# Scores gathered with the token rows, experts' inner rows weighted by them, and the six picked rows added without weights

## The reference, cut to what matters

```python
logits = xf @ w_router                     # 1024 tokens x 32 experts
scores = sigmoid(logits)
...                                        # 6 of 32 experts are picked by scores + corr_bias
# per picked expert e: y_e = (silu(x @ gate_w[e]) * (x @ up_w[e])) @ down_w[e]   (inner width 176)
# out = sum over the six picks of scores[e] * y_e, plus a shared expert (inner width 352)
x = x + gb * out
```

## Time and profile before

| | us |
|---|---|
| median of 3 runs | 437.58 |
| lowest, highest | 435.03, 437.88 |
| the profiled execution | 438.39 |
| span of its instructions | 436.6 |

### The profile page before, as it was taken

The page is one execution under the profiler, slowest core; times in us unless marked ns, Lnnn a source line. Parts: engine busy times, 40 slices in busy tenths (PEclk is TensorE's granted clock), DMA queues, the critical chain, the costliest instruction groups (busy, mean ns, idle before and its releaser), DMA issues. The chain is left out here.

```text
span 436.6 us, 6170 instructions
## 1 busy us (share of the span) xinstructions
PE 407.1 (93%) x1923; PEld 306.7 (70%) x1924; DVE 286.3 (66%) x693; ACT 201.8 (46%) x380; POOL 129.3 (30%) x143
## 2 busy tenths in 40 slices
PE   6996898988999999999999899899899979999997
PEld 6463748455777777777776647687587858798886
DVE  4898885887444444444444476989677998985542
ACT  2578825482222222222222247482896397613430
POOL 1000020004777777777777500701000010010000
PEclk9999696968999999999999989999999989999999
DMA  8996667981323233333238259902400000001001
GB/s 278 413 389 135 149 148 179 360 373 41 104 98 107 98 108 96 107 96 110 96 106 276 87 189 376 359 12 44 172 2 0 2 1 0 2 2 48 2 0 49
DMA packets 24010, 56.89 MB, mean 130 GB/s; under 512 B 4528, under 2 KB 15794, under 8 KB 22996
## 3 DMA queue, kind: packets, MB, share of 16 engines
q1 hardware_dynamic: 18564, 41.80, 28.7%
q0 software_dynamic: 5424, 14.82, 10.3%
HBM read 46.10 MB, written 10.50 MB: 130 GB/s over the span
## 5 line engine op out<-in xcount | busy, mean ns | idle before, releaser
L736 PE MATMUL bank<-arena,tile_mem 128*128 x224 | 75.6, 460 | 0.0
L1411 POOL DMA_INDIRECT tile_mem<-h_dram,gidx x57 | 56.0, 982 | 53.8 <-DVE gidx L1779 36.8
L1399 POOL TENSOR_TENSOR rstd<-ve,mhalf 128x2 f32<-128x2 f32 (+1 forms) x14 | 11.3, 806 | 185.9 <-DVE ve L1539 185.9
L1418 POOL DMA_INDIRECT y_dram<-norm,didx x56 | 55.3, 988 | 21.8 <-issue 13.7
L1795 DVE TENSOR_TENSOR tile_mem<-tile_mem,bank 128x176 f32<-128x176 f32 x56 | 18.9, 338 | 62.3 <-ACT tile_mem L1209 62.3
L752 PE MATMUL bank<-arena,tile_mem 88*128 x224 | 57.7, 379 | 0.8 <-DVE tile_mem L1790 0.8
L752 PEld LDWEIGHTS bank<-arena,tile_mem 88*128 88x128 f32 x224 | 42.4, 190 | 15.7 <-issue 1.0
L847 PE MATMUL bank<-x_r,f_r 128*128 128x512 f32 x192 | 46.4, 402 | 0.7 <-DVE x_r L1975 0.6
L736 PEld LDWEIGHTS bank<-arena,tile_mem 128*128 128x128 f32 x224 | 38.3, 191 | 11.8
L1209 ACT ACTIVATE tile_mem<-bank 128x176 f32<-128x176 f32 x56 | 17.8, 317 | 57.5 <-PE bank L736 57.5
L847 PEld LDWEIGHTS bank<-x_r,f_r 128*128 128x128 f32 x192 | 36.8, 193 | 9.8 <-issue 0.8
(11 more groups left out here) (281 smaller groups left out, 722.0 us busy)
## 6 DMA issues: line engine op xcount, KB each, us to landing
arena<-w_gu SPq DMA_DIRECT2D x3, 2112.0 KB, 12.3
arena<-w_dn SPq DMA_DIRECT2D x4, 1408.0 KB
arena<-w_gu SPq DMA_DIRECT2D x2, 2464.0 KB, 20.5
arena<-y_dram SPq DMA_DIRECT2D x6, 768.0 KB, 8.2
arena<-w_f SPq DMA_DIRECT2D x6, 512.0 KB, 7.8
arena<-wmod SPq DMA_DIRECT2D x3, 512.0 KB, 9.3
arena<-wmod SPq DMA_DIRECT2D x2, 768.0 KB, 11.0
arena<-y_dram SPq DMA_DIRECT2D x4, 384.0 KB, 4.5
```

Of the source, the lines that this page charges most:

```text
L736: mm = pe.matmul(bank[2 + r % 2][:, 0:2 * M], xgT[r % 2][:, k * P:(k + 1) * P], gu[:, bass.ds(e[k], 2 * M)], start=(k == 0), stop=(k == CT ...
L1411: pool.indirect_dma_start(out=xg[j % 4], out_offset=None, in_=h2_dram, in_offset=bass.IndirectOffsetOnAxis(ap=gidx[:, j:j + 1].bitcast(U32 ...
L1418: pool.indirect_dma_start(out=y_dram, out_offset=bass.IndirectOffsetOnAxis(ap=didx[:, j:j + 1].bitcast(U32), axis=0), in_=yt[j % 4], in_of ...
```

## The change

Five things, all in layer 0's mixture of experts:

1. A row of `h2_dram` is longer by 32 numbers: SP writes the 32 scores of each token behind its 256 channels with a second DMA per sequence, and what waits for h2 waits for both. A gather brings 288 numbers instead of 256.
2. `tile_hidden` becomes a scalar_tensor_tensor that also multiplies by the score of the tile's expert. That score is one column of the gathered row, and which column is held in a register: VectorE loads four registers from `eoff` at the head of each quad, as PE does.
3. A gather into a used buffer waits for `hid_ready` instead of `tx_done`, since the scores in it are read until then.
4. `wk`, its twelve instructions, ScalarE's `choice_parts` and PE's `choice_sums` go. VectorE adds the picked rows itself, without weights: for token tiles 0 and 1 together (`first_picks`, `other_picks`), for the others one tile at a time (`all_picks`).
5. SP reads the residual rows X2 ahead of its wait for the last scatter, not behind the picks.

Some buffers move (`pidx` and `pint` into others, the four `yg` buffers into one). The diff, cut to its core:

```diff
-    h2_dram = nc.dram_tensor("h2_dram", (B * S, C), F32, kind="Internal").ap()
+    h2_dram = nc.dram_tensor("h2_dram", (B * S, C + E), F32, kind="Internal").ap()
...
+                sp_.wait_ge(score_ready, b + 1)
                 sp_.wait_ge(h2_ready, b + 1)
-                sp_.dma_start(h2v[:, b * TB:(b + 1) * TB, :], norm[:, b * TB:(b + 1) * TB, :]).then_inc(h2_out, 16)
+                sp_.dma_start(h2v[:, b * TB:(b + 1) * TB, 0:C], norm[:, b * TB:(b + 1) * TB, :]).then_inc(h2_out, 16)
+                sp_.dma_start(h2v[:, b * TB:(b + 1) * TB, C:XR], scores[:, b * TB:(b + 1) * TB, :]).then_inc(h2_out, 16)
...
+            for b in range(B):
+                half = slice(b * TB * C, (b + 1) * TB * C)
+                sp_.dma_start(X2.rearrange("p t c -> p (t c)")[:, half], x1_dram[:, half]).then_inc(x1_in[b], 16)
             for i in range(4):
                 sp_.wait_ge(y_out[i], 16 * last_q + 16)
...
-            for t in range(TB):
-                choice_sums(t)
             pe.wait_ge(shhid_ready, 2 * SHT)
             shared_out(1, (2, 3), range(TB))
...
-            act.wait_ge(wk_ready, 1)
-            shared_silu(1, ms=range(2))
-            choice_parts(0)
-            choice_parts(1)
-            shared_silu(1, ms=range(2, SHT))
-            choice_parts(2)
-            choice_parts(3)
+            shared_silu(1)
...
                 if j >= 4:
-                    pool.wait_ge(tx_done, j - 3)
+                    pool.wait_ge(hid_ready, j - 3)
...
+            regs = [dve.alloc_register(f"score{i}") for i in range(4)]
             def tile_hidden(q, r):
+                e = dve.snap(regs[r], min_val=0, max_val=E - 1)
                 dve.wait_ge(sil_ready, 4 * q + (r + 1))
-                tt(hid[r % 2], sil[r % 2], bank[2 + r % 2][:, M:2 * M], ALU.mult).then_inc(hid_ready, 1)
+                stt(hid[r % 2], sil[r % 2], xg[r][:, bass.ds(e + C, 1)], bank[2 + r % 2][:, M:2 * M], ALU.mult, ALU.mult)\
+                    .then_inc(hid_ready, 1)
...
             def quad(q, first=False):
+                dve.load(regs, eoff[0:1, bass.ds(4 * q + 1, 4)])
                 for r in range(4):
...
+            def first_picks():
+                acc = shared_y[:, 0:2, :]
+                for t in range(2):
+                    dve.wait_ge(yg_half[t], 16)
+                for k in range(TOPK // 2):
+                    step(tt(acc, acc, yg_pair[:, :, k, :], ALU.add))
+                    settle()
...
+            def all_picks(t):
+                y, half = yg[t % YG], TOPK // 2
+                dve.wait_ge(yg_in[t % YG], 16 * (t // YG + 1))
+                step(tt(y[:, 0:half, :], y[:, 0:half, :], y[:, half:TOPK, :], ALU.add))
+                settle()
+                step(tt(y[:, 0, :], y[:, 0, :], y[:, 1, :], ALU.add))
+                step(tt(shared_y[:, t, :], shared_y[:, t, :], y[:, 2, :], ALU.add))
+                settle()
+                step(tt(shared_y[:, t, :], shared_y[:, t, :], y[:, 0, :], ALU.add))
+                settle()
...
-            half_sums(range(2))
-            shared_hidden(1, range(1, SHT))
-            half_sums(range(2, TB))
-            gated_sums(range(2))
-            gated_sums(range(2, TB))
+            first_picks()
+            shared_hidden(1, range(1))
+            other_picks()
+            shared_hidden(1, range(1, 2))
+            gated_sums(0, 1)
             variance(4, x2, (0,), stats_done=True)
-            variance(4, x2, (1,))
+            all_picks(2)
+            shared_hidden(1, range(2, SHT))
+            all_picks(3)
+            gated_sums(2, 3)
+            variance(4, x2, (1,), stats_done=True)
             normalise(4, x2)
```

134 lines of the change are left out of this document (40 added, 94 removed).

## The result

| | before | after |
|---|---|---|
| median (lowest to highest), us | 437.73 (435.03 to 441.12) | 456.27 (456.06 to 457.13) |
| the profiled execution, us | 438.39 | 456.39 |
| its span, us | 436.6 | 454.6 |

The change makes the kernel slower: the ratio is 1.043 (95% interval 1.038 to 1.048). The forecast was 452.0 us, with a range of 443 to 460.

What follows compares the result with a forecast made beforehand. PE was taken to set the pace. The loop's 11.1 us (6.5 for loads, 4.6 for tiles) and 2.4 behind it add 13.5 to the profiled 438.4, giving 452 us, range 443 to 460.

Steps and rivals of the forecast that it cites:

- The load at the border: Loop, start of each quad: VectorE's four-register load delays `copy_h` by 0.5 us, 13 times, 6.5 us in all.
- the bounds are 0.336 and 0.551, I take 0.40, near the same load: Loop, quad border: VectorE's load takes 0.40 us, between PE's load of the same table and VectorE's one load.
- I count no cover: Loop, quad border: none of the late `copy_h` is hidden before PE's down projection load, 0.2 us at most.
- Tile by tile: Loop, `tile_hidden`: register operation 0.09 and longer product 0.06, less 0.04 to spare, 0.11 us in 42 tiles, 4.6 us.
- The room at `th`: Loop: the chain gate/up, silu, `tile_hidden`, `th` has about 0.04 us to spare per tile.
- The gathers: Loop, POOL: gathers waiting for `tile_hidden` keep up with the tiles and cost 0 us (-1.0 to +1.5).
- Behind the loop: From loop to layer 1: PE's saved 6.8 us become waiting, the clock falls, and the transposes start 2.4 us later (1 to 5).
- I add 0.5 for the landing: Behind the loop: the first picks land 0.5 us later (0 to 2), as residual reads run beside the last scatter.
- 3 us at half rate cost 1.5: Behind the loop, `shared_out`: PE's clock, lowered after idling, costs 1.5 us.
- (a): Loop, quad border: rival that VectorE's register load is hidden, giving 447 us; chance 0.2.
- (b): Loop: rival that POOL's gathers at 2.56 us per tile set the pace, giving 445 us; chance 0.1.
- (c): Loop: rival that room at `th` and the down projection makes the loop cost nothing, not slower, 438 us; chance 0.1.

Runs made afterwards that it cites:

- run 2: Kernel before plus VectorE's load of four registers at each quad's head, each register used for a one-column copy behind `copy_h`: 448.95 us, ratio 1.026.
- run 4: Kernel after, score column copied ahead behind each `copy_h`, releasing the gather's buffer; next quad's registers loaded in the quad's last tile: 443.70 us, ratio 1.013.
- run 3: Kernel after without VectorE's register loads and the register operation; the product always reads column 256, so the score's choice is left out: 445.75 us, ratio 1.012.
- first form of run 2: Kernel before plus the four-register load with registers unused; the compiler left the load out, leaving one wait ahead of the loop: 439.27 us, ratio 1.000.
- run 6: Kernel after with SP's reads of the residual rows X2 moved back behind the picks, as in the kernel before: 456.66 us, ratio 1.040.
- run 1: Kernel after with VectorE's load of four registers moved from ahead of the quad's first `copy_h` to behind it: 447.51 us, ratio 1.015.
- run 9: Kernel after with the column copied ahead, the load moved, and picks split without weights, VectorE two and PE four for four token tiles: 439.54 us, ratio 1.004.
- run 10: Kernel after, column copied ahead, silu wait on the product, picks split three and three, one `shared_out` tile ahead of PE's second wait: 438.89 us, ratio 1.0005.
- run 5: Kernel after with the column copied ahead and load moved, the wait for the silu written ahead of that for the column: 442.49 us, ratio 1.013.
- run 8: Kernel after with VectorE adding two picks of token tiles 0 to 3, PE four, without weights; residual reads behind the picks: 454.28 us, ratio 1.036.

## Why the prediction was right, and where its sizes were wrong

The sign, the place (the loop most of it) and four mechanisms hold: the load stands in the way of `copy_h`, the register operation and the longer product lengthen the tile, PE's saved sums become waiting, and the clock falls in that wait. The time is 4.3 us above the forecast, because two terms were too small, the load and the end. Some of the nearness is luck: errors within the terms cancelled, and the first stretch gave back 1.5 us that the change has no part in.

- **The load at the border**: forecast 13 x 0.5 = 6.5, a step near 3.0; measured 12 steps of 3.17 to 3.43, 10.6 in all. The order of events was right (the load started once `copy_y` had started, not during its wait, and `copy_h` came behind it), and so was PE's wait for `copy_h`. What failed is the step "the bounds are 0.336 and 0.551, I take 0.40, near the same load": the load took 0.97 to 1.15 us, above both bounds. PE's load of the same table and VectorE's load of one register were no bounds for VectorE's load of four. "I count no cover" was wrong the other way: `copy_h` came 1.23 us later behind `copy_y` (1.68 for 0.45), and the step grew by 0.92 (3.41 for 2.49), so 0.3 were covered, near the 0.27 of the earlier trace rows. In run 2 it is 1.10 and 0.85.
- **Tile by tile**: forecast 42 x 0.11 = 4.6, measured 42 steps that are 3.7 longer in sum, 0.09 each. Close, but two parts were off and cancelled in part. The operation cost 0.11 on the chain, not 0.09. The product's 0.06 was right. The room at `th` is about 0.08, not 0.04: in after the chain is 0.17 longer and the step 0.09, in run 4 0.13 (0.07 + 0.06) and 0.05 on the average, and in run 3 the product's 0.06 alone fits in (steps of 2.49).
- **The gathers**: forecast 0 (-1.0 to +1.5), measured +1.0 in one step, which the first form of run 2 has too, so none of it is shown to be the change's. They became the bound only where the tiles were brought back to 2.49 with the release by `hid_ready` (run 3). The wider rows cost nothing that the traces show: a gather lands 2.8 us (median) after its issue in both kernels.
- **Behind the loop**: forecast +2.4 (by its own figures 2.7, since VectorE was to end at 278.7 and the transposes had started at 276.05), measured +4.5 in this pair of profiles. VectorE's chain from the first picks to `shared_out` was worked out at 12.0 and is 12.1 (274.74 to 286.85). The step "I add 0.5 for the landing" measured 1.9 (9.05 behind `shared_in` for 7.17): SP's picks began 4.0 us after POOL's last scatter was issued, 2.2 before, and run 6 shows that the residual reads are the reason. The step "3 us at half rate cost 1.5" measured 2.2: the low clock lasted 10 us, 4.2 of them in `shared_out`. PE's idle time ahead of it, 7.6 us by the forecast (264.1 to 271.7), was 10.6, since `shared_in` ran at the full clock and was done 1.5 earlier, and `shared_out` began 2.3 us later against it instead of 0.8.
- **Rivals**: (a), the load hidden, falls in after, but is what run 1 makes of it by moving it one instruction. The queue rule of the Trainium skill ("Perfetto Trace Analysis", section "DVE / Act Engine Instruction (TENSOR_ADD, Activation, etc)"), by which it would have been hidden where it stood, is contradicted by run 2: the load started 0.4 us behind the start of the copy that had waited (124.8, 124.39), and the border took 0.85 us more. The floor of about 0.6 us for a tensor_load in "DMA: Bandwidth & Descriptors" of the Trainium skill, section "Latency and other measured facts", agrees with VectorE's 0.97 to 1.15 as a floor, and not with PE's 0.336 or VectorE's 0.551 for one register. (b) needs tiles at 2.49 and came inside the loop in run 3 alone. (c) did not come: PE waited for `copy_h` at twelve of thirteen borders and stood behind the product in the ordinary tiles.

Runs 9 and 10 tell what is left when most of the two costs is taken away: 0.4% and 0.05%, no gain. In run 9 PE does 40 products in the sums where it did 32 before, in run 10 again 32. ScalarE's busy time falls from 201.8 us to 196.7 in run 9, VectorE's from 286.3 to 284.6, beside a PE that is busy for 94% of the span. That this saving is worth nothing because it lies beside PE is argued from these shares; no run shows it by itself.

What stays open: how long the load takes on VectorE by number of registers (only loads of one and of four were seen), and why it took 1.13 us in after and 0.97 in runs 1 and 2. Its place isn't the reason: in run 2 it stands where it stands in after, and in run 5, behind `copy_h`, five of 14 took 1.16 to 1.21.

## What to carry to other kernels

A register load, an address worked out from a register, and the second of two waits are work of an engine's sequencer, in the order of its program. In a loop where the engine waits for somebody in every turn, put them behind an instruction that is followed by such a wait, not behind the wait: there a load of 1 us cost nothing (run 1), and on the other side 0.07 us cost 0.02 to 0.06 in every turn (run 4). When two chains end together, shortening one moves the wait to the other; what helped here was dividing the work anew.

## What the runs showed that was not expected

- A load of four registers takes 0.97 to 1.15 us on VectorE in after, PE's load of the same table 0.336.
- Of two waits ahead of one instruction, one stands on the instruction and the other on a semaphore operation of 21 ns ahead of it; which is which followed the order in which they were written, and with the late one on the operation the tile was 0.02 to 0.06 us longer (runs 4 and 5).
- A load whose registers nobody reads is not in the program that runs (run 2), so the cost of a load can't be measured that way.
- The lower clock falls in different places in different executions: with the same 1.0 us of idle time ahead of it, `shared_in` took 10.56 us at a granted clock of 1.00 in after, and 12.10 at 0.50 for its first 3 us in before. In run 8 it took 13.29. Up to 2.7 us of a difference between two profiles in this stage can be that.
